# Row scatters of an expert-routing kernel issued in pairs and one by one, each behind a semaphore

## The chip, the cores and the metric

The kernel runs on one core of one Trainium2 chip. The metric is the device time of one execution in microseconds (us). A core has five engines with an instruction queue each: TensorE (PE: matmuls and transposes, with the weight loads shown as PEld), VectorE (DVE), ScalarE (ACT), GpSimd (POOL) and SyncE (SP, which here only issues plain DMAs). Engines wait for each other through semaphores.

## The reference, cut to what matters

```python
h = tok(x)                                      # patches of x times W, plus b: 128 x 92 tokens of 128
h = h + attention(layernorm(h), Wq, Wk, Wv, Wlt)
t = layernorm(h)
gates = softmax(t @ Wr + br)                    # 8 experts
top_vals, top_idx = top_k(gates, 2)             # two experts for each token, weights made to sum to 1
out = zeros_like(t)
for e in range(8):
    y = relu(t @ W1[e] + b1[e]) @ W2[e] + b2[e] # 128 -> 512 -> 128
    out = out + combine[:, e:e + 1] * y         # combine is zero but for a token's two experts
h = h + out
```

There are T = 11,776 tokens of D = 128 floats.

## The kernel before

It has four stages, one behind the other.

**Stage one** embeds and makes the attention, group by group.

**Stage two** walks over 23 chunks of 512 tokens (`NCH`). A chunk's eight blocks of attention output are turned by TensorE into four PSUM banks (`turn_a`, L1743), copied by ScalarE (`keep_aTh`, L980, semaphore `aTh_kept`), of six of them VectorE makes the rounding rest (`keep_aTl`, L1248), and TensorE projects them (L401 to L403, L1752). VectorE adds the residual (`keep_h1`, L1258; the trace calls its result `h`), TensorE turns the result to token rows with the router's columns beside it (`turn_h`, L1764), ScalarE keeps logits, residual and squares, GpSimd takes the power -1/2 of the variance (`root2`, L828, semaphore `rstd2_kept`), and VectorE does some 25 small routing steps that end in `posi`, the row of each token's two copies in an array sorted by expert. GpSimd then scatters the normalised rows `trow` to that array in DRAM (`scatter`, L835): eight indirect DMAs for a chunk (two choices times four row blocks), each of 128 rows. While chunk c is routed, TensorE already projects chunk c+1, and the scatters under way are those of chunk c-1.

**Stage three** walks over 53 tiles (`TILES`) of 512 sorted rows, seven of them of 256 rows (`HALF_TILES`). For each, `turn_tile` (L1780) and `keep_x`, `low_x` bring the rows in, `first_layer` makes four pieces of the hidden layer, ScalarE keeps each piece's high half (`keep_hid`, L1028) and VectorE its low half (`low_hid`, L1391, semaphore `hidl_kept`, four for a tile), `second_layer` multiplies them, `turn_y` (L1845) turns the result, VectorE weighs it (`weigh_y`, L1540, the trace's `ytok`), and GpSimd scatters it by token (L862): four indirect DMAs for a tile, two for a half one. The second half of tile n's work on TensorE is interleaved with the first of tile n+1.

**Stage four** loads the two results of each token and adds them.

The order on every engine is the order of the code: nothing is scheduled. GpSimd's queue in a step of stage two is: scatters 0 and 1 of chunk c-1, `root2(c)`, scatters 2 to 7 of chunk c-1. `pool_waits` is a helper that makes GpSimd wait for the semaphores given and then counts up one of its own.

Of the kernel before, what the change touches and what calls it, by code (L numbers as in the profile page):

```python
# [19 lines left out]
FC = FF // P  # L20
# [19 lines left out]
NCH = T // CT  # L40
RT = CT // P
# [4 lines left out]
AC = H * D // P  # L46
# [34 lines left out]
READY = 9  # L81
BY_DVE = tuple(c for c in range(NCH) if c not in BY_TENSOR)
TABLE_SET = 9
assert 2 * T % TT == 0 and T % CT == 0 and GT <= 512 and HH * S == GT and H * S * D == S * H * D


def at_least(eng, sem, value):

    if isinstance(value, int) and value <= 0:
        return  # L90
    eng.wait_ge(sem, value)
# [10 lines left out]
def rows_of_tile(n):  # L102

    return HT // P if isinstance(n, int) and n in HALF_TILES else TR
# [21 lines left out]
def build(nc, x, tok_w, tok_b, wq, wk, wv, wlt, wr, br, w1, b1, w2, b2, out):  # L126
# [9 lines left out]
    with ExitStack() as ctx, nc.allow_non_contiguous_dma("biases once"):  # L136
# [3 lines left out]
        def sem(name):  # L140
            return ctx.enter_context(nc.semaphore(name))
# [31 lines left out]
        last = ExitStack()  # L173
# [25 lines left out]
        first = ExitStack()  # L199
# [163 lines left out]
        aT_done, aTh_kept, aTl_kept, proj_done, h1_kept = (sem(n) for n in (  # L363
            "aT_done", "aTh_kept", "aTl_kept", "proj_done", "h1_kept"))
        wrc_done, wrc_kept, lean_kept, square_kept, var2_kept, rstd2_kept, shift_kept = (sem(n) for n in (
            "wrc_done", "wrc_kept", "lean_kept", "square_kept", "var2_kept", "rstd2_kept", "shift_kept"))
        route, mask_kept, gap_kept, gapexp_kept, count_done, posi_kept = (sem(n) for n in (
            "route", "mask_kept", "gap_kept", "gapexp_kept", "count_done", "posi_kept"))
        trow_kept, res_done, res_kept, goal_kept = (sem(n) for n in (
            "trow_kept", "res_done", "res_kept", "goal_kept"))  # L370
# [9 lines left out]
        hid_done, hidh_kept, hidl_kept, part_done = (sem(n) for n in ("hid_done", "hidh_kept", "hidl_kept", "part_done"))  # L380
# [39 lines left out]
        def steps_second(eng, chunk):  # L420

            chunk(0, 0, 0, True)
            for n in range(NE // 2):
                chunk(2 * n + 1, n, 1, True)
                chunk(2 * n + 2, n + 1, 0, True)
            with eng.Fori(NE // 2, (NCH - 3) // 2) as i:
                chunk(2 * i + 1, i, 1, True)
                chunk(2 * i + 2, i + 1, 0, True)
            chunk(NCH - 2, (NCH - 3) // 2, 1, True)
            chunk(NCH - 1, (NCH - 1) // 2, 0, False)  # L430
# [14 lines left out]
        def is_tile(n):  # L445
            return not isinstance(n, int) or 0 <= n < TILES

        def pool_waits(*waits):


            for sm, v in waits:
                at_least(nc.gpsimd, sm, v)
            nc.gpsimd.sem_inc(passed, 1)
# [200 lines left out]
        def _(pool):  # L654
# [143 lines left out]
            def set_table():  # L798

                for ins in (pool.iota(thresholds[:], pattern=[[HT, UNITS]], base=0, channel_multiplier=0,  # L800
                                      allow_small_or_imprecise_dtypes=True),
                            pool.iota(full_no[:], pattern=[[1, FULLS]], base=0, channel_multiplier=0,
                                      allow_small_or_imprecise_dtypes=True),
                            pool.iota(half_no[:], pattern=[[1, HALVES]], base=0, channel_multiplier=0,
                                      allow_small_or_imprecise_dtypes=True),
                            pool.iota(to_split[:], pattern=[[-2, 3]], base=HALVES - 2, channel_multiplier=0,
                                      allow_small_or_imprecise_dtypes=True),
                            pool.iota(star_row[:], pattern=[[TT, STAR]], base=0, channel_multiplier=0,
                                      allow_small_or_imprecise_dtypes=True),
                            pool.memset(len_line[:, 0:SEGS], 0.0),  # L810
                            pool.memset(seg_start[:, SEGS:SEGS + 1], float(SPARE_ROW)),
                            pool.iota(seg_step[:].rearrange("o (a e) -> o a e", a=2), pattern=[[0, 2], [0, NE]], base=1,
                                      channel_multiplier=0, allow_small_or_imprecise_dtypes=True)):
                    ins.then_inc(table_set, 1)
                pool.wait_ge(table_set, TABLE_SET - 1)
                ins = pool.iota(seg_step[:, NE - 1:SEGS:NE], pattern=[[NE - 1, 2]], base=1 - NE, channel_multiplier=0,
                                allow_small_or_imprecise_dtypes=True)
                ins.then_inc(table_set, 1)

            def lay_spare(k):  # L820
                row = SPARE_ROW + k * TT
                pool.dma_start(sorted_dram[row:row + TT, :].rearrange("(p r) w -> p r w", p=P),
                               spare_rows[:, k]).then_inc(spares_in, 16)

            def root2(c, q):

                pool_waits((var2_kept, c + 1), (trow_kept, 2 * c - 2), (mask_kept, c - 1))
                nc.gpsimd.tensor_tensor(rstdB[:, q], varB[:], power[:], ALU.pow).then_inc(rstd2_kept, 1)  # L828

            def scatter(c, q, first, last):  # L830

                if first == 0:
                    pool_waits((trow_kept, 2 * c + 2), (posi_kept, c + 1))
                for choice, r in [(k // RT, k % RT) for k in range(first, last)]:
                    pool.indirect_dma_start(  # L835
                        out=sorted_dram, out_offset=bass.IndirectOffsetOnAxis(ap=posi[:, q, choice, r:r + 1], axis=0),
                        in_=trow[:, q, choice, r], in_offset=None).then_inc(scattered[q], 16)

            def chunk(c, i, q, more):

                after_first = not isinstance(c, int) or c > 0
                if after_first:
                    scatter(c - 1, 1 - q, 0, 2)
                root2(c, q)
                if after_first:
                    scatter(c - 1, 1 - q, 2, 2 * RT)
                if isinstance(c, int) and c < SPARE:
                    lay_spare(c)
                if isinstance(c, int) and c == NE:
                    set_table()  # L850

            steps_second(pool, chunk)
            scatter(NCH - 1, (NCH - 1) % 2, 0, 2 * RT)

            def tile(n, i, q):
                m = n - 1
                if is_tile(m):
                    b = (q - 1) % XRING
                    pool_waits((tile_in[b], 16 * ((m // XRING if isinstance(m, int) else i - int(q == 0)) + 1)),
                               (ytok_kept, m + 1))  # L860
                    for r in range(rows_of_tile(m)):
                        pool.indirect_dma_start(  # L862
                            out=y_dram, out_offset=bass.IndirectOffsetOnAxis(ap=tin[:, b, r, D:D + 1].bitcast(I32), axis=0),
                            in_=ytok[:, b % 2, r], in_offset=None).then_inc(y_out[b % 2], 16)

            tiles(pool, tile)

        @block.scalar
# [245 lines left out]
        def _(dve):  # L1114
# [246 lines left out]
            def nxt(ins):  # L1361
                lined[0] += 1
                ins.then_inc(ready_kept, 1)
                dve.wait_ge(ready_kept, lined[0])
# [4 lines left out]
            def choose_star():  # L1369

                dve.wait_ge(table_set, TABLE_SET)
                nxt(V.tensor_reduce(best[:, 0:1], held[:], AX_X, ALU.max))
# [551 lines left out]
```

## Time and profile before

| | |
|---|---|
| median of 3 runs | 1600.33 us (1600.16 to 1606.58) |
| span of the profiled execution, first to last instruction | 1622.7 us |
| TensorE busy | 1443.9 us (89%) |
| VectorE, ScalarE, GpSimd busy | 73%, 62%, 49% |

The profiled execution has no time of its own beside its span. The span is 22.4 us over the median of the unprofiled runs. Busy shares are means over four stages. A bracket at the end of a row of the timeline says how long the engine had been idle ahead of that instruction and what ended it.

### The profile page before, as it was taken

What the parts mean: (1) busy time and instruction counts of PE and PEld (TensorE: products, weight loads), DVE (VectorE), ACT (ScalarE), POOL (GpSimd) and SP (SyncE); (2) the same over time, 40 slices, a digit from 0 to 9 for tenths busy, and PEclk for the clock granted to TensorE, in tenths of its full rate; (3) what the DMA queues carried; (4) which work ended last, traced back from release to release, by engine and by line L of the source; (5) the groups of instructions that cost most, each with busy time, mean ns of one, the idle gap of its engine ahead of it and who ended that gap; (6) DMA issues with size and microseconds to landing.
All of it is one profiled execution on the core that took longest, in us unless ns stands there. A gap on an engine that the chain in (4) does not pass through costs nothing.

```text
span 1622.7 us, 31484 instructions
## 1 busy us (share of the span) xinstructions
PE 1443.9 (89%) x7812; PEld 1155.4 (71%) x7812; DVE 1184.5 (73%) x3231; ACT 1008.0 (62%) x2311; POOL 788.2 (49%) x888
## 2 busy tenths in 40 slices
PE   5999999999999999999988878787858899998894
PEld 4778888888888888888766656565646777777671
DVE  3988989989989988988957666556756455555455
ACT  2777878878878878878855655455534444444350
POOL 2674444444444444444416665555654445445451
PEclk8999999999999999999999998888979989999996
DMA  3422222222222222222366664546446666655579
GB/s 83 138 85 78 97 83 81 92 84 82 90 84 86 86 84 87 85 84 88 125 236 216 229 218 163 194 148 207 140 161 224 231 232 224 210 203 207 194 255 364
DMA packets 135458, 245.74 MB, mean 151 GB/s; under 512 B 31536, under 2 KB 95552, under 8 KB 132448
## 3 DMA queue, kind: packets, MB, share of 16 engines
q1 hardware_dynamic: 114608, 206.57, 36.7%
q0 software_dynamic: 13920, 31.33, 5.8%
q10 hardware_dynamic: 6864, 7.09, 1.3%
q8 instruction: 27, 0.44, 0.1%
q14 instruction: 39, 0.32, 0.1%
HBM read 99.85 MB, written 89.51 MB: 117 GB/s over the span
## 4 chain that ended last, share of the span: by engine, by line
PE 73%; DVE 6%; issue 6%; another core or an unknown queue 5%; ACT 4%; DMA 2%; POOL 2%; SPq 1%; ACTq 0%; POOLq 0%; DVEq 0%
PE bank L401 15%; PE bank L403 14%; PE bank L402 13%; PE pair_ps L1678 9%; PE bank L1609 5%; PE bank L1703 4%; PE bank L1743 4%; PE pair_ps L1845 1%; PE pair_ps L1764 1%; PE bank L1599 1%; ACT trow L1003 1%; ACT aT_h L980 1%; PE bank L1752 1%; DMA yearly<-y_scratch 1%
## 5 line engine op out<-in xcount | busy, mean ns | idle before, releaser
L692 POOL TENSOR_TENSOR prob<-expo,inv 92x368 f32<-92x368 f32 x256 | 205.0, 801 | 394.4 <-DVE inv L1207 394.4
L862 POOL DMA_INDIRECT y_scratch<-ytok,tin x198 | 194.3, 981 | 189.5 <-issue 126.3
L835 POOL DMA_INDIRECT sorted_scratch<-trow,posi x184 | 180.2, 979 | 124.8 <-issue 87.2
L1678 PE MATMUL pair_ps<-z,xnT 128*92 128x368 f32 x512 | 201.4, 475 | 0.0
L1391 DVE SCALAR_TENSOR_TENSOR hid_l<-bank,hid_h 128x512 fp32r<-128x512 f32 (+1 forms) x159 | 103.7, 655 | 118.7 <-ACT hid_h L1028 69.3
L1200 DVE TENSOR_REDUCE peak<-pair_ps 92x4 f32<-92x368 f32 x256 | 136.1, 532 | 73.1 <-PE pair_ps L1678 72.9
L1248 DVE TENSOR_TENSOR aT_l<-bank,aT_h 128x512 fp32r<-128x512 f32 x138 | 94.9, 691 | 90.3 <-ACT aT_h L980 67.4
L902 ACT ACTIVATE z<-bank 128x368 f32<-128x368 f32 x254 | 121.2, 477 | 63.3 <-PE bank L403 56.0
L1028 ACT ACTIVATE hid_h<-bank 128x512 fp32r<-128x512 f32 (+1 forms) x159 | 90.6, 570 | 105.1 <-PE bank L403 73.9
L941 ACT ACTIVATE w2s<-bank 128x368 fp32r<-128x368 f32 x256 | 122.5, 479 | 47.2 <-PE bank L403 42.4
L948 ACT ACTIVATE expo<-cent 92x368 f32<-92x368 f32 x256 | 130.4, 509 | 31.1 <-DVE cent L1212 28.2
L1227 DVE TENSOR_TENSOR w2s<-bank,w2s 128x368 fp32r<-128x368 f32 x256 | 136.2, 532 | 5.9 <-ACT w2s L941 3.0
L1212 DVE TENSOR_TENSOR cent<-pair_ps,peak 92x368 f32<-92x368 f32 x256 | 136.4, 533 | 1.0
L1220 DVE TENSOR_TENSOR probT_l<-bank,probT_h 92x368 fp32r<-92x368 f32 x256 | 134.9, 527 | 1.8 <-ACT probT_h L929 1.8
L980 ACT ACTIVATE aT_h<-bank 128x512 fp32r<-128x512 f32 x138 | 83.7, 609 | 81.2 <-PE bank L1743 46.6
L1193 DVE TENSOR_REDUCE total<-expo 92x4 f32<-92x368 f32 x256 | 133.4, 521 | 0.4 <-ACT expo L948 0.3
L957 ACT ACTIVATE val<-bank 128x368 f32<-128x368 f32 x256 | 120.6, 471 | 17.0 <-PE bank L403 12.8
L1743 PEld LDWEIGHTS bank<-ident,arow 128*128 128x128 f32 x736 | 98.4, 151 | 42.1 <-issue 27.0
L401 PE MATMUL bank<-probT_h,xtok_h 92*128 92x368 f32 x256 | 114.1, 446 | 10.4 <-DVE w2s L1227 7.3
L1703 PE MATMUL bank<-ident,prob 92*92 92x92 f32 x1024 | 123.0, 242 | 0.3 <-POOL prob L692 0.3
L929 ACT ACTIVATE probT_h<-bank 92x368 fp32r<-92x368 f32 x256 | 119.7, 468 | 0.3
L1743 PE MATMUL bank<-ident,arow 128*128 128x128 f32 x736 | 119.4, 290 | 0.0
(274 smaller groups left out, 3972.7 us busy)
## 6 DMA issues: line engine op xcount, KB each, us to landing
ax_scratch<-val SPq DMA_DIRECT2D x64, 736.0 KB, 3.5
arow<-ax_scratch SPq DMA_DIRECT2D x23, 2048.0 KB
w1t<-w1s SPq DMA_DIRECT2D x53, 512.0 KB
w2t<-w2s SPq DMA_DIRECT2D x53, 512.0 KB
tin<-sorted_scratch SPq DMA_DIRECT2D x46, 260.0 KB
xin<-in_x_dram SPq DMA_DIRECT2D x32, 372.0 KB
ywide<-y_scratch SPq DMA_DIRECT2D x32, 256.0 KB, 6.7
h_scratch<-hP SPq DMA_DIRECT2D x32, 184.0 KB, 5.1
```

Of the source, the lines that this page charges most:

```text
L401: mm(dst, wh, vh, start=start, stop=False)
L402: mm(dst, wh, vl, start=False, stop=False)
L403: return mm(dst, wl, vh, start=False, stop=stop)
L692: nc.gpsimd.tensor_tensor(prob[:, k % 2], expo[:, k % 2], inv[:, k % 2].unsqueeze(2).to_broadcast([S, HH, S]), ALU.mult).then_inc(prob_kep ...
L835: pool.indirect_dma_start(out=sorted_dram, out_offset=bass.IndirectOffsetOnAxis(ap=posi[:, q, choice, r:r + 1], axis=0), in_=trow[:, q, ch ...
L862: pool.indirect_dma_start(out=y_dram, out_offset=bass.IndirectOffsetOnAxis(ap=tin[:, b, r, D:D + 1].bitcast(I32), axis=0), in_=ytok[:, b % ...
L1200: V.tensor_reduce(peak[:, k % 2], sc, AX_X, ALU.max).then_inc(peak_kept, 1)
L1212: V.tensor_tensor(cent[:, k % 2], sc, peak[:, k % 2].unsqueeze(2).to_broadcast([S, HH, S]), ALU.subtract).then_inc(cent_kept, 1)
L1227: V.tensor_tensor(mix_l[:, half * HH:(half + 1) * HH, b, :], mix_ps[:, 0:GT].rearrange("d (h i) -> d h i", h=HH), mix_h[:, half * HH:(half ...
L1678: mm(score_ps[k % 2][0:S, 0:GT], xnT[:, q, b * S:(b + 1) * S], z[:, b, half * HH:(half + 1) * HH, :], start=True, stop=True).then_inc(scor ...
L1703: ins = nc.tensor.transpose(probT_ps[kt % 2][0:S, m * S:(m + 1) * S], prob[:, kt % 2, m], ident[0:S, 0:S])
L1743: ins = nc.tensor.transpose(turn_ps[j % TURNS][:, r * P:(r + 1) * P], arow[q][:, r, j * P:(j + 1) * P], ident[:])
```

## The change

Every `scatter` after the first of a chunk now waits for something, and a chunk's last six are cut in three pairs:

```diff
@@ -81,6 +81,7 @@
+NEXT_LOW = {1: 0, 2: 1, 3: 2}
@@ -827,30 +828,36 @@
-            def scatter(c, q, first, last):
-
-                if first == 0:
-                    pool_waits((trow_kept, 2 * c + 2), (posi_kept, c + 1))
+            def scatter(c, q, first, last, *after):
+
+                pool_waits(*(after if first else ((trow_kept, 2 * c + 2), (posi_kept, c + 1))))
                 for choice, r in [(k // RT, k % RT) for k in range(first, last)]:
                     pool.indirect_dma_start(
                         out=sorted_dram, out_offset=bass.IndirectOffsetOnAxis(ap=posi[:, q, choice, r:r + 1], axis=0),
                         in_=trow[:, q, choice, r], in_offset=None).then_inc(scattered[q], 16)
 
             def chunk(c, i, q, more):
+
+                def turned(blocks):
+                    blocks += AC * (c + 1)
+                    return aTh_kept, min(blocks, AC * NCH) if isinstance(c, int) else blocks
 
                 after_first = not isinstance(c, int) or c > 0
                 if after_first:
                     scatter(c - 1, 1 - q, 0, 2)
                 root2(c, q)
                 if after_first:
-                    scatter(c - 1, 1 - q, 2, 2 * RT)
+                    scatter(c - 1, 1 - q, 2, 4, (rstd2_kept, c + 1))
+                    scatter(c - 1, 1 - q, 4, 6, turned(AC))
+                    scatter(c - 1, 1 - q, 6, 8, turned(AC + 1))
...
             steps_second(pool, chunk)
-            scatter(NCH - 1, (NCH - 1) % 2, 0, 2 * RT)
+            for k in range(0, 2 * RT, 2):
+                scatter(NCH - 1, (NCH - 1) % 2, k, k + 2, (hidl_kept, FC + k // 2))
@@ -859,6 +866,8 @@
                     for r in range(rows_of_tile(m)):
+                        if r in NEXT_LOW and is_tile(n + 1):
+                            pool_waits((hidl_kept, FC * (n + 1) + NEXT_LOW[r]))
                         pool.indirect_dma_start(
                             out=y_dram, out_offset=bass.IndirectOffsetOnAxis(ap=tin[:, b, r, D:D + 1].bitcast(I32), axis=0),
                             in_=ytok[:, b % 2, r], in_offset=None).then_inc(y_out[b % 2], 16)
```

`AC` is 8, the blocks of a chunk: `turned(AC)` is the moment when ScalarE has kept all eight blocks of chunk c+1, `turned(AC + 1)` that when it has kept the first of chunk c+2. `FC` is 4: `FC * (n + 1)` low halves are all of tile n, so a tile m = n - 1 has its second scatter behind the last low half of tile n, its third and fourth behind the first and second of tile n+1. No instruction of any other engine changes.

GpSimd's queue in the last two steps of stage two, of before (`trow` are the rows, `sorted_scratch` the sorted array, `rstdB` the result of `root2`):

```order
L835 DMA sorted_scratch<-trow,posi 101888x130 [waits trow_kept,posi_kept]
L835 DMA sorted_scratch<-trow,posi 101888x130
L828 TENSOR_TENSOR rstdB<-varB,power 128x4 [waits mask_kept,var2_kept,trow_kept]
L835 DMA sorted_scratch<-trow,posi 101888x130 x6
L835 DMA sorted_scratch<-trow,posi 101888x130 [waits trow_kept,posi_kept]
```

and of the same step in the changed kernel:

```order
L835 DMA sorted_scratch<-trow,posi 101888x130 [waits trow_kept,posi_kept]
L835 DMA sorted_scratch<-trow,posi 101888x130
L829 TENSOR_TENSOR rstdB<-varB,power 128x4 [waits mask_kept,var2_kept,trow_kept]
L835 DMA sorted_scratch<-trow,posi 101888x130 [waits rstd2_kept]
L835 DMA sorted_scratch<-trow,posi 101888x130
L835 DMA sorted_scratch<-trow,posi 101888x130 [waits aTh_kept]
L835 DMA sorted_scratch<-trow,posi 101888x130
L835 DMA sorted_scratch<-trow,posi 101888x130 [waits aTh_kept]
L835 DMA sorted_scratch<-trow,posi 101888x130
L835 DMA sorted_scratch<-trow,posi 101888x130 [waits trow_kept,posi_kept]
```

The instructions stand in the same order; the run of six without a wait has become three pairs with a wait each.

GpSimd's queue where stage two ends and the tiles begin, of before (`ytok` are a tile's weighed rows, `y_scratch` the array of results by token):

```order
L835 DMA sorted_scratch<-trow,posi 101888x130 [waits trow_kept,posi_kept]
L835 DMA sorted_scratch<-trow,posi 101888x130 x7
L862 DMA y_scratch<-ytok,tin 31232x128 [waits tile_in0,ytok_kept]
L862 DMA y_scratch<-ytok,tin 31232x128 x3
L862 DMA y_scratch<-ytok,tin 31232x128 [waits tile_in1,ytok_kept]
```

and of the changed kernel:

```order
L835 DMA sorted_scratch<-trow,posi 101888x130 [waits trow_kept,posi_kept]
L835 DMA sorted_scratch<-trow,posi 101888x130
L835 DMA sorted_scratch<-trow,posi 101888x130 [waits hidl_kept]
L835 DMA sorted_scratch<-trow,posi 101888x130
L835 DMA sorted_scratch<-trow,posi 101888x130 [waits hidl_kept]
L835 DMA sorted_scratch<-trow,posi 101888x130
L835 DMA sorted_scratch<-trow,posi 101888x130 [waits hidl_kept]
L835 DMA sorted_scratch<-trow,posi 101888x130
L871 DMA y_scratch<-ytok,tin 31232x128 [waits tile_in0,ytok_kept]
L871 DMA y_scratch<-ytok,tin 31232x128 [waits hidl_kept] x3
L871 DMA y_scratch<-ytok,tin 31232x128 [waits tile_in1,ytok_kept]
```

The last chunk's eight scatters, one run of before, now stand in pairs behind low halves of tile 1, and each of a tile's later scatters has a wait of its own.

## Rows read from the trace of the kernel before

**Rows 1.** Single lines: count, shortest, median and longest ns, first and last start.

```profile
L835 POOL DMA_INDIRECT sorted_scratch<-trow,posi x184: 965/972/1070, 851.6 to 1205.9; - x184
L1258 DVE TENSOR_TENSOR h<-bank,hch x23: 680/682/692, 836.9 to 1175.1; 128x512 f32<-128x512 f32 x23
L1540 DVE TENSOR_TENSOR ytok<-pair_ps,tin x53: 415/681/693, 1202.2 to 1582.6; 128x512 f32<-128x512 f32 x46, 128x256 f32<-128x256 f32 x7
```

**Rows 2.** Timeline, first chunks: start, us, engine, line, operation.

```profile
846.49 1.02 PE L1752 MATMUL bank<-aT_f,wlt_f 128*128 128x512 f32 x2
848.24 0.68 DVE L1258 TENSOR_TENSOR h<-bank,hch 128x512 f32<-128x512 f32 x1
```

**Rows 3.** Timeline of a later chunk, its scatters and what waits.

```profile
984.42 0.68 DVE L1258 TENSOR_TENSOR h<-bank,hch 128x512 f32<-128x512 f32 x1
...
988.96 0.97 POOL L835 DMA_INDIRECT sorted_scratch<-trow,posi  x1 [0.30 <-issue]
...
990.75 1.00 PE L1743 MATMUL bank<-ident,arow 128*128 128x128 f32 x4
...
991.79 0.60 ACT L980 ACTIVATE aT_h<-bank 128x512 fp32r<-128x512 f32 x1 [0.78 <-PE bank L1743]
...
992.75 1.02 POOL L835 DMA_INDIRECT sorted_scratch<-trow,posi  x1 [0.20 <-issue]
...
995.20 0.60 ACT L980 ACTIVATE aT_f<-bank 128x512 f32<-128x512 f32 x1 [0.53 <-issue]
...
996.55 0.60 PE L1743 MATMUL bank<-ident,arow 128*128 128x128 f32 x4
...
996.99 1.02 PE L1752 MATMUL bank<-aT_f,wlt_f 128*128 128x512 f32 x2
...
999.18 0.97 POOL L835 DMA_INDIRECT sorted_scratch<-trow,posi  x1 [0.30 <-issue]
1000.04 0.60 ACT L980 ACTIVATE aT_h<-bank 128x512 fp32r<-128x512 f32 x1 [2.43 <-PE bank L1743]
...
1001.41 0.69 DVE L1258 TENSOR_TENSOR h<-bank,hch 128x512 f32<-128x512 f32 x1
...
1002.34 2.17 PE L1764 MATMUL pair_ps<-turnw,h 128*128 128x137 f32 x8 [3.26 <-DVE h L1258]
```

**Rows 4.** Timeline where stage two ends: the last scatter of a row of twelve, and ScalarE.

```profile
1211.02 0.97 POOL L862 DMA_INDIRECT y_scratch<-ytok,tin  x1 [0.30 <-issue]
1211.96 0.60 ACT L1028 ACTIVATE hid_h<-bank 128x512 fp32r<-128x512 f32 x1 [7.19 <-remote]
```

**Rows 5.** Timeline of an undisturbed tile: weighed rows, a low half, the last scatter.

```profile
1345.32 0.68 DVE L1540 TENSOR_TENSOR ytok<-pair_ps,tin 128x512 f32<-128x512 f32 x1
...
1349.13 0.69 DVE L1391 SCALAR_TENSOR_TENSOR hid_l<-bank,hid_h 128x512 fp32r<-128x512 f32 x1 [0.68 <-ACT hid_h L1028]
...
1350.61 0.97 POOL L862 DMA_INDIRECT y_scratch<-ytok,tin  x1 [0.30 <-issue]
...
1351.72 0.68 DVE L1540 TENSOR_TENSOR ytok<-pair_ps,tin 128x512 f32<-128x512 f32 x1
```

**Rows 6.** Timeline of a disturbed tile.

```profile
1409.18 0.40 PE L403 MATMUL pair_ps<-x_both,w1t 128*128 128x512 f32 x1
...
1409.43 0.69 DVE L1540 TENSOR_TENSOR ytok<-pair_ps,tin 128x512 f32<-128x512 f32 x1
...
1410.92 0.96 POOL L862 DMA_INDIRECT y_scratch<-ytok,tin  x1 [1.12 <-issue]
...
1411.62 0.60 ACT L1028 ACTIVATE hid_h<-pair_ps 128x512 fp32r<-128x512 f32 x1 [3.12 <-PE bank L403]
...
1414.74 0.97 POOL L862 DMA_INDIRECT y_scratch<-ytok,tin  x1 [0.30 <-issue]
...
1416.04 0.69 DVE L1391 SCALAR_TENSOR_TENSOR hid_l<-bank,hid_h 128x512 fp32r<-128x512 f32 x1 [1.51 <-issue]
...
1419.36 0.68 DVE L1540 TENSOR_TENSOR ytok<-pair_ps,tin 128x512 f32<-128x512 f32 x1
```

## The prediction, made before the changed kernel ran

> **What bounds the kernel now.** I read the page, then single lines for the periods of the two loops, then the timeline around one chunk and two tiles. TensorE is busy for 89% of the span, so the question is what stops it in the rest. In stage two `keep_h1` ran 23 times from 836.9 to 1175.1 [rows 1], 338.2 / 22 = 15.4 us a chunk. Its first period, which held no scatter, took 848.24 - 836.9 = 11.3 us [rows 1, 2]. From there to the last are 326.9 us for 21 periods, 15.6 us each, 4.2 us over the first. In stage three `ytok` ran 53 times from 1202.2 to 1582.6 [rows 1], while an undisturbed tile takes 1351.72 - 1345.32 = 6.40 us [rows 5]. With 45 full periods at 6.4 and 7 half ones at 3.2, halved as the width is, the floor is 310 us for 380.4: 70 us over.
>
> The timeline shows where a chunk loses it. At 984.42 to 1001.41 (17.0 us) TensorE's last projection ends by its record at 996.99 + 1.02 = 998.01, and the `h` that waits for it starts at 1001.41, 3.4 us late; TensorE then had been idle 3.26 us when `turn_h` began. The turned block that ends at 996.55 + 0.60 = 997.15 reaches ScalarE at 1000.04, with ScalarE idle for 2.43 us of that [rows 3]. Without scatters the same projection ends at 847.51 and `h` starts at 848.24, 0.7 us later [rows 2]. What is late is not the work but the word of it: two engines that wait for TensorE are released together long after its record ends. GpSimd was in a run of six scatters, first at 992.75, last at 999.18 [rows 3], one each 1.28 us (0.97 and a gap of 0.30); `h` starts 2.2 us after the last one's start. Behind a pair nothing is late: the second scatter of a pair starts at 988.96, the block turned until 991.75 is taken up at 991.79 [rows 3]. Stage three has the same picture: a row of twelve scatters ends with that of 1211.02, and ScalarE stands 7.19 us until 1211.96 [rows 4]; `L403` ends by its record at 1409.58, ScalarE takes it up at 1411.62 [rows 6], 2.0 us late, behind a run of four. So I read: **after several scatters in close order TensorE's signals come late, until about 2.2 us after the last scatter starts; after two they don't.** The profile shows it as coincidence in time, not as a cause.
>
> **The change part by part.** The same 382 scatters are issued, of 0.972 us each [rows 1]. No data moves differently. What is added are waits and a count on GpSimd, three a chunk and up to three a tile. Its queue has room: it is busy for 49% of the span. Where a wait is already met it costs a queue instruction that hides behind the running scatter. Where it binds, the restart costs more: `ytok` ends at 1410.12 and its scatter starts at 1410.92 [rows 6], 0.8 us, against 0.30 between two in a run, so 0.5 us a binding wait, on an engine with slack. Behind a waiting scatter on GpSimd stand the chunk's other scatters and the next `root2`, for which ScalarE and VectorE wait a third of a period later.
>
> Chunk, pair two (behind `root2`): its wait is for the instruction just ahead, so I cost it at nothing, 0.5 us at most. Pair three, behind the last block kept: `aT_f` of 995.20 ends at 995.80 [rows 3], so it starts at 996.6 where its first scatter stands at about 995.35 by that spacing: 1.2 us later, and a gap of 2.5 instead of 1.3 in the run. Pair four waits for the block that ScalarE took at 1000.04; if the signal isn't late, that block is kept by about 998.3 (ScalarE is free at 1000.04 - 2.43 = 997.61, plus 0.60), and the pair starts at 999.1 instead of 997.90; if it is late, the run has stopped after four and the release comes 2.2 us after the fourth's start of 997.9, so at 1000.1 instead of 1001.4. Either way `h` can start earlier: by 1.3 us at least by that rule, and by 1001.41 - 998.8 = 2.6 us when nothing is late (0.7 us behind 998.01, as in [rows 2]). Above lies the whole excess of 4.2 us a chunk, below nothing, if the last pair, now next to the following chunk's first pair, makes a run of four with it and gives the gain back there. I take 1.5 us, near the lower of the two: the last pair still falls near `turn_h`. For 21 chunks **31 us** (0 to 88).
>
> The last chunk's scatters and tile 0's: the row of twelve goes. ScalarE's stop of 7.19 us becomes one of about 2: **5 us** (0 to 7).
>
> Tiles: in the undisturbed one the waits do nothing. The low half for which the fourth scatter would wait ends at 1349.13 + 0.69 = 1349.82; 0.8 us on is 1350.62, and the scatter starts at 1350.61 already [rows 5]. In the disturbed tile, 1409.43 to 1419.36 or 9.9 us, the fourth scatter started at 1414.74, while the low half it would wait for ended at 1416.73 [rows 6]: it would start at 1417.5, 2.8 us later, and the run of four, hard behind the one before, is broken up by waits that follow TensorE's own progress. I take it that a third to a quarter of the 70 us comes back: 3.5 us over the floor in such a tile, half of it regained, in some ten such tiles, 16 to 18: **16 us** (0 to 50, the rest belongs to the half tiles and to what starts a disturbance, which no wait touches).
>
> Sum 31 + 5 + 16 = 52 us off the profiled span of 1622.7, so 1571. The median stands 22.4 us under the span; I take the same 52 off it: **1548 us**. If late signals are shorter without the profiler, the gain is smaller; that stretches the range up.
>
> **The rivals.**
> *Smaller gain (1575 to 1592).* The signals stay late in most chunks: pairs two and three are still four scatters between 992.75 and 998.9, and pair four comes early in chunks at full clock. Then 0.5 to 1 us a chunk and little in the tiles: about 15 to 20 us, 1583.
> *No change (about 1600).* Late signals come from something else that happens to coincide, and the scatters merely stand nearby. For it speaks that no semaphore of GpSimd's is what TensorE waits for; against it, that chunks without scatters show none of it. Then only GpSimd waits longer: 1600. "Trainium Architecture — The Big Picture", section "What this means for kernel authors", in the Trainium skill says that the engines are independent and that one blocks another only through a semaphore, and that inside SBUF only VectorE and GpSimd share a port. By that rule a scatter can't delay TensorE's word to ScalarE, and the sum would be 0 and the time 1600. The trace speaks against it so far, with 3.4 us late behind six scatters and 0.7 us without.
> *Slower (about 1621).* The last pair of chunk c-1 now starts behind the first block of the next step, so around `h` of that step, and the first pair of chunk c follows `posi` some 2.5 us later: four in close order just where ScalarE waits for `turn_h` to make logits and squares. Those feed `root2`, and behind `root2` stand six scatters and all routing. If each chunk loses 1 us there beyond what it gains, that is 21 us: 1621. It decides from the point where the late word of `turn_h` costs more than the 3.4 us that `h` loses now. Against it: those two pairs are 2 us or more apart if the signal isn't late, and `turn_h` ends between them.
>
> **How the numbers follow.** Forecast, 1518 to 1575: 0.58. Smaller gain: 0.15. No change: 0.13. Slower: 0.14. A measurement of this kernel tells about 0.5% (8 us) from no change. The point is the forecast's, 1548. Its own range is 1518 to 1575, from 82 us off (two thirds of the 88 and a third of the 70) to 25. For 8 in 10 the range goes up to no change and leaves the slower case out: 1518 to 1602. Faster by over 0.5% takes the first two: 0.73; within 0.5% 0.13; slower 0.14.
>
> **What would show it.** In the changed kernel's profile: `keep_h1` less than 1.5 us behind TensorE's last projection in most chunks and a mean period of 14 us (23 starts in about 305 us); TensorE's granted clock less often halved in stage two, as its stops shrink; ScalarE's stop of 7 us at the stages' seam gone; tiles of over 9 us rare, and `ytok` from first to last in about 360 us; undisturbed tiles still 6.40. Wrong it would be if signals are as late with pairs as with six, if the lateness moves from `h` to the logits behind `turn_h`, or if unprofiled runs never had it.

## The result, and the profile after

The changed kernel took 1591.35 us (median of 20 runs, 1579.98 to 1598.63) where the kernel before took 1604.77 us in its 20 runs (1593.92 to 1614.0): a ratio of 0.992, 95% interval 0.990 to 0.994. So 13.4 us came back where 52 were forecast. It is faster, as forecast, but by a quarter of the amount, and outside the forecast's range of 1518 to 1575 us.

Two numbers of the forecast's ground look different now. The profiled execution of before that was read ahead of the prediction has a span of 1622.7 us, above every one of these 20 runs of before; a second profiled execution of the same kernel has 1597.6. And the profiled execution of after is the fastest of its 20. Comparing these two traces overstates the gain, so each kernel has a second trace below. The second traces come from two chips, on which the kernel before took 1601.29 (before_again's chip) and 1604.54 us (after_again's); on which chip the first trace of before was taken is not on record.

The page of the changed kernel, first lines (busy us, share of the span, instructions).

```profile
span 1578.2 us, 31768 instructions
PE 1421.0 (90%) x7812; PEld 1136.6 (72%) x7812; DVE 1181.5 (75%) x3231; ACT 1004.8 (64%) x2311; POOL 787.9 (50%) x888
```

Single lines of the changed kernel, beside [rows 1]. The diff moves the line numbers by 9 at `h` and `ytok`.

```profile
L835 POOL DMA_INDIRECT sorted_scratch<-trow,posi x184: 962/972/1068, 849.3 to 1196.1; - x184
L1267 DVE TENSOR_TENSOR h<-bank,hch x23: 678/680/681, 834.5 to 1168.2; 128x512 f32<-128x512 f32 x23
L1549 DVE TENSOR_TENSOR ytok<-pair_ps,tin x53: 411/681/693, 1190.6 to 1538.4; 128x512 f32<-128x512 f32 x46, 128x256 f32<-128x256 f32 x7
```

The scatters cost what they did. `h` runs over 333.7 us, 15.2 us a chunk, and `ytok` over 347.8. The same lines in the second traces, first of before, then of after:

```profile
L1258 DVE TENSOR_TENSOR h<-bank,hch x23: 680/681/692, 834.5 to 1158.3; 128x512 f32<-128x512 f32 x23
L1540 DVE TENSOR_TENSOR ytok<-pair_ps,tin x53: 415/681/692, 1184.9 to 1557.4; 128x512 f32<-128x512 f32 x46, 128x256 f32<-128x256 f32 x7
```

```profile
L1267 DVE TENSOR_TENSOR h<-bank,hch x23: 679/680/683, 839.2 to 1176.1; 128x512 f32<-128x512 f32 x23
L1549 DVE TENSOR_TENSOR ytok<-pair_ps,tin x53: 414/682/692, 1203.2 to 1552.6; 128x512 f32<-128x512 f32 x46, 128x256 f32<-128x256 f32 x7
```

In the second pair the chunks are slower with the change, 336.9 / 22 = 15.3 us against 323.8 / 22 = 14.7, and the tiles faster, 349.4 us against 372.5. In the first pair the chunks looked a little quicker (333.7 us against 338.2), because that trace of before is the longer of its two. Whether the two halves of the change pull against each other is tried below, one half at a time.

A chunk of the changed kernel (timeline, weight loads and small VectorE rows left out) shows where the chunk's loss stands.

```profile
995.71 0.97 POOL L835 DMA_INDIRECT sorted_scratch<-trow,posi  x1 [1.22 <-ACT aT_f L989]
996.98 0.97 POOL L835 DMA_INDIRECT sorted_scratch<-trow,posi  x1 [0.30 <-issue]
...
997.93 0.68 DVE L1267 TENSOR_TENSOR h<-bank,hch 128x512 f32<-128x512 f32 x1
998.26 0.96 POOL L835 DMA_INDIRECT sorted_scratch<-trow,posi  x1 [0.30 <-ACT aT_h L989]
...
998.85 1.17 PE L1773 MATMUL pair_ps<-turnw,h 128*128 128x137 f32 x8 [0.67 <-DVE h L1267]
...
999.53 0.97 POOL L835 DMA_INDIRECT sorted_scratch<-trow,posi  x1 [0.30 <-issue]
...
1001.28 0.96 POOL L835 DMA_INDIRECT sorted_scratch<-trow,posi  x1 [0.79 <-DVE posi L1355]
...
1002.55 0.97 POOL L835 DMA_INDIRECT sorted_scratch<-trow,posi  x1 [0.30 <-issue]
1003.01 0.20 ACT L995 ACTIVATE lgraw<-pair_ps 128x36 f32<-128x36 f32 x1 [4.75 <-remote]
...
1004.34 0.69 DVE L1257 TENSOR_TENSOR aT_l<-bank,aT_h 128x512 fp32r<-128x512 f32 x1 [3.21 <-remote]
...
1005.09 0.50 PE L402 MATMUL bank<-aT_h,wlt_h 128*128 128x512 f32 x1 [2.49 <-DVE aT_l L1257]
```

`h` no longer waits, and TensorE is idle for 0.67 us ahead of `turn_h`, where [rows 3] had 3.26. But `turn_h` ends by its record at 998.85 + 1.17 = 1000.02, and ScalarE takes it up (`lgraw`) at 1003.01, 3.0 us late, with ScalarE idle for 4.75 and VectorE for 3.21 us. The trace also holds the times at which semaphores are counted up: the count of `turn_h` comes at 1002.90. TensorE's next blocks start at 1000.56 and 1001.99, before that, so it is the word (the semaphore's count, which ScalarE waits for) that is late. The ends of matmuls in a profile are modelled, though; whether the last write of `turn_h` was late with its word no run here tells. Pairs three and four have run together to four scatters, 995.71 to 999.53, and the next chunk's first pair follows 0.79 us behind them. The late word has moved from `h` to the logits.

Where the tiles begin, ScalarE's longest stop is now 4.25 us where [rows 4] had 7.19 (timeline of the changed kernel, ScalarE alone):

```profile
1190.66 0.60 ACT L1037 ACTIVATE hid_h<-pair_ps 128x512 fp32r<-128x512 f32 x1 [3.44 <-PE pair_ps L404]
...
1199.65 0.60 ACT L1031 ACTIVATE x_both<-bank 128x512 fp32r<-128x512 f32 x1 [4.25 <-remote]
...
1203.99 0.60 ACT L1037 ACTIVATE hid_h<-pair_ps 128x512 fp32r<-128x512 f32 x1 [3.75 <-PE bank L404]
```

But only the first of the last chunk's pairs stands apart (same timeline, GpSimd alone):

```profile
1186.77 0.97 POOL L835 DMA_INDIRECT sorted_scratch<-trow,posi  x1 [0.30 <-issue]
1189.71 0.97 POOL L835 DMA_INDIRECT sorted_scratch<-trow,posi  x1 [1.98 <-DVE hid_l L1400]
1190.98 0.97 POOL L835 DMA_INDIRECT sorted_scratch<-trow,posi  x1 [0.30 <-issue]
1192.26 0.97 POOL L835 DMA_INDIRECT sorted_scratch<-trow,posi  x1 [0.30 <-issue]
...
1201.19 0.97 POOL L871 DMA_INDIRECT y_scratch<-ytok,tin  x1 [0.30 <-issue]
1205.36 1.09 POOL L871 DMA_INDIRECT y_scratch<-ytok,tin  x1 [3.20 <-DVE hid_l L1400]
```

The second pair waits for its low half, and by then the low halves of all that follow are there: from 1189.71 to 1201.19 ten scatters run 1.28 us apart, the other six of the chunk and tile 0's four. The row of twelve has become two and ten. The first four periods of `ytok`, which hold this place, take 38.8 and 38.0 us in the two traces of before and 35.7 in both of the changed kernel.

An undisturbed tile still takes 1488.96 - 1482.56 = 6.40 us, with its scatters now 1.60, 1.27 and 1.27 us apart (timeline, `ytok` and scatters of one tile):

```profile
1482.56 0.68 DVE L1549 TENSOR_TENSOR ytok<-pair_ps,tin 128x512 f32<-128x512 f32 x1
...
1484.02 0.97 POOL L871 DMA_INDIRECT y_scratch<-ytok,tin  x1 [1.25 <-issue]
...
1485.62 0.97 POOL L871 DMA_INDIRECT y_scratch<-ytok,tin  x1 [0.64 <-issue]
...
1486.89 0.97 POOL L871 DMA_INDIRECT y_scratch<-ytok,tin  x1 [0.30 <-issue]
...
1488.16 0.97 POOL L871 DMA_INDIRECT y_scratch<-ytok,tin  x1 [0.31 <-issue]
...
1488.96 0.68 DVE L1549 TENSOR_TENSOR ytok<-pair_ps,tin 128x512 f32<-128x512 f32 x1
```

Of the 52 periods from `ytok` to `ytok` 3 are over 8.5 us, where the two traces of before have 13 and 17.

### The profile page after: what moved, and what is told of

Its sections match the earlier page's. It is cut to its first block, busy times and chain, and to the rows that moved or that the text cites. A ratio compares the mean times of both kernels' runs of the same rounds, so it can differ in the third digit from the quotient of the medians.

```text
span 1578.2 us, 31768 instructions
## 1 busy us (share of the span) xinstructions
PE 1421.0 (90%) x7812; PEld 1136.6 (72%) x7812; DVE 1181.5 (75%) x3231; ACT 1004.8 (64%) x2311; POOL 787.9 (50%) x888
## 4 chain that ended last, share of the span: by engine, by line
PE 73%; DVE 8%; issue 7%; ACT 4%; another core or an unknown queue 4%; DMA 2%; POOL 1%; SPq 1%; ACTq 0%; DVEq 0%; POOLq 0%
PE bank L402 16%; PE bank L404 14%; PE bank L403 14%; PE pair_ps L1687 9%; PE bank L1618 5%; PE bank L1712 5%; PE bank L1752 3%; PE pair_ps L1854 1%; PE bank L1608 1%; ACT trow L1012 1%; PE bank L1789 1%; ACT aT_h L989 1%; DMA yearly<-y_scratch 1%; DVE aT_l L1257 1%
## 5 line engine op out<-in xcount | busy, mean ns | idle before, releaser
L402 PE MATMUL bank<-aT_h,wlt_h 128*128 128x512 f32 x138 | 73.1, 530 | 54.2 <-DVE aT_l L1257 41.8
```

What stands on the lines that cost most here:

```text
L402: mm(dst, wh, vh, start=start, stop=False)
```

## The experiments

Two kernels are no experiments but second looks at before and after, for the reading above. Each ratio is to runs of the kernel before that were taken with it.

**before_again.** 

> The kernel before, unchanged, for a second trace. If the first trace (span 1622.7 us) is a typical execution, chunks again take 15.4 us and ytok again runs over about 380 us. If it is an unusually slow one, which its distance to the median says, the span is about 1603 us and the difference lies in the tiles or the chunks: ytok from first to last in 360 to 370 us.

It took 1599.37 us, with a span of 1597.6, 25 us under the first trace. The chunks make up 14 of these; `ytok` from first to last, 372.5 us, lies a little above what was expected.

**after_again.** 

> The changed kernel again, for a second trace: h about 0.8 us behind the last projection, logits over 4 us behind h, chunks 15.2 us or more, ytok from first to last 345 to 360 us; span 1585 to 1595 us.

It took 1594.63 us (span 1592.8), and all else came as expected: `h` 0.8 us behind the last projection, the logits 4.6 us behind `h`, chunks of 15.3 us, tiles in 349.4.

**One half of the change at a time.** In chunks_only, tiles and last chunk scatter as before; in tiles_only, the chunks do:

```diff
 # chunks_only keeps these two places as before
-            for k in range(0, 2 * RT, 2):
-                scatter(NCH - 1, (NCH - 1) % 2, k, k + 2, (hidl_kept, FC + k // 2))
+            scatter(NCH - 1, (NCH - 1) % 2, 0, 2 * RT)
...
-                        if r in NEXT_LOW and is_tile(n + 1):
-                            pool_waits((hidl_kept, FC * (n + 1) + NEXT_LOW[r]))
 # tiles_only keeps this one as before
-                    scatter(c - 1, 1 - q, 2, 4, (rstd2_kept, c + 1))
-                    scatter(c - 1, 1 - q, 4, 6, turned(AC))
-                    scatter(c - 1, 1 - q, 6, 8, turned(AC + 1))
+                    scatter(c - 1, 1 - q, 2, 2 * RT)
```

**chunks_only.** 

> Only the waits of stage two's chunks; last chunk and tiles as before. Theory A: GpSimd's scatters are worked off slower (about 1.5 us each) than a run issues them (1.28 us), TensorE's signals wait behind a run of three and more, and the pairs of the change close up to such runs again at another place, so the lateness moved from h to the logits. Then the chunks take 15.0 to 15.3 us and the time is 0 to 5 us under the kernel before (ratio 0.997 to 1.000). Theory B: the pairs gain in the chunks as forecast and the tiles are what gave it back: ratio 0.98.

**tiles_only.** 

> Only the waits of the last chunk and of the tiles; the chunks as before. Theory A: nearly all of the measured 13 us is here: ratio 0.991 to 0.995, ytok from first to last about 350 us in the profile. Theory B: no gain here: ratio 1.000 or above.

Measured: chunks_only 1616.86 us against 1601.29, ratio 1.008 (1.005 to 1.011). tiles_only 1574.42, ratio 0.983 (0.979 to 0.988). Single lines of `h` and `ytok`, first chunks_only, then tiles_only:

```profile
L1264 DVE TENSOR_TENSOR h<-bank,hch x23: 680/681/682, 838.5 to 1178.6; 128x512 f32<-128x512 f32 x23
L1546 DVE TENSOR_TENSOR ytok<-pair_ps,tin x53: 415/681/693, 1205.5 to 1579.4; 128x512 f32<-128x512 f32 x46, 128x256 f32<-128x256 f32 x7
```

```profile
L1266 DVE TENSOR_TENSOR h<-bank,hch x23: 680/681/692, 836.4 to 1163.6; 128x512 f32<-128x512 f32 x23
L1548 DVE TENSOR_TENSOR ytok<-pair_ps,tin x53: 415/681/692, 1186.4 to 1531.9; 128x512 f32<-128x512 f32 x46, 128x256 f32<-128x256 f32 x7
```

By these ratios the chunks' part costs 0.8%, 12.5 us (the interval says 8 to 18), and the tiles' part with the last chunk's gives 1.7%, 27 us (20 to 34). Together 14.5, which fits the 13.4 measured: the two halves do pull against each other. Neither expectation had chunks_only slower than before, and tiles_only was expected to gain half as much. tiles_only alone beats both kernels.

**Spacing alone, in the order of before.** Behind every scatter, in chunks and tiles, GpSimd clears a small tile of its own, which nobody reads; order and waits stay those of before. The whole output is computed.

```diff
+            def space(done):
+                pool_waits((idled, done))
+                pool.memset(idle[:], 0.0).then_inc(idled, 1)
...
                         in_=trow[:, q, choice, r], in_offset=None).then_inc(scattered[q], 16)
+                    space(2 * RT * c + RT * choice + r)
```

The tile has 160 floats in spaced, 280 in spaced_mid, 400 in spaced_wide and 640 in spaced_more.

**spaced.** 

> The kernel before with no wait of the change; instead GpSimd clears 160 floats of one partition (about 0.25 us) behind every scatter, so that scatters start 1.5 to 1.6 us apart instead of 1.28 and their order and place stay. Theory A (they are worked off in about 1.5 us each, and the signals are late only when they pile up): no late signals, undisturbed tiles of 6.4 us throughout, chunks of about 14 us bounded by GpSimd, 1540 to 1570 us. Theory C (each scatter delays signals whatever its distance, or their number counts): the same lateness over a longer run of scatters, chunks of 17 us, 1610 to 1640 us.

**spaced_mid.** 

> The scatters' order of before, with a memset of 280 floats behind each scatter, for starts about 1.46 us apart, between the 1.37 us of the kernel spaced (ratio 0.990) and the 1.56 us of spaced_wide (0.968). Theory (each scatter is worked off in about 1.47 us, and a run issued faster than that builds a backlog behind which TensorE's signals wait): the backlog all but vanishes at 1.46, so most of the gain is there, 0.970 to 0.978, 1556 to 1569 us. Rival (the gain only follows the spacing evenly, with no point at which it turns): halfway between the two, 0.979, 1571 us. Rival (a run of six is late because it is one run, unless it is slower by more than the DMA's own time): as spaced, 0.988 to 0.992.

**spaced_wide.** 

> As spaced, but GpSimd clears 400 floats, 0.42 us by the 0.22 us that 160 took. In spaced the starts came 1.37 us apart, closer than 1.47 us, in which the trace shows a scatter of a run worked off (runs of six released 8.75 us after their start at spacings of 1.28 and of 1.37 alike). Now they come about 1.56 us apart. Theory A: nothing piles up, TensorE's signals are late by under 0.5 us, chunks take about 13.5 us, undisturbed tiles 6.40 us, no tile over 8.5 us; 1535 to 1560 us. Theory C (the number of scatters in a row counts, whatever their spacing): the lateness stays and lasts 9.4 us a run; chunks 15 us, 1590 to 1610 us.

**spaced_more.** 

> The same with a memset of 640 floats, starts about 1.75 us apart. Theory: there is no backlog to take away beyond 1.56 us, so the ratio stays at 0.965 to 0.972, unless GpSimd itself becomes late: eight scatters then take 14.0 us, which is the whole period of a chunk (13.8 us), so routing and root2 are late and a chunk takes 14.5 to 15 us: 1565 to 1580 us, ratio 0.975 to 0.985. I take the latter. Rival (gain grows evenly with spacing): 0.95, 1524 us.

Measured, with the start to start of two scatters of a run:

| | spacing | us | ratio (95%) | a chunk | `ytok`, first to last |
|---|---|---|---|---|---|
| before_again | 1.28 | 1599.37 | | 14.7 | 372.5 |
| spaced | 1.37 | 1586.88 | 0.990 (0.986 to 0.993) | 14.0 | 378.7 |
| spaced_mid | 1.47 | 1577.96 | 0.985 (0.981 to 0.990) | 14.2 | 360.7 |
| spaced_wide | 1.56 | 1551.97 | 0.968 (0.964 to 0.972) | 13.8 | 342.2 |
| spaced_more | 1.77 | 1590.02 | 0.994 (0.991 to 0.997) | 15.3 | 349.9 |

spaced was expected at 1540 to 1570 us, and missed it: its clears set the scatters only 1.37 us apart, not 1.5 to 1.6. With 1.56 us, in spaced_wide, GpSimd was given more to do and the kernel got 3.2% faster. Timeline of spaced_wide, around one `h`:

```profile
1007.22 0.98 POOL L841 DMA_INDIRECT sorted_scratch<-trow,posi  x1 [0.17 <-POOL idle L834]
...
1008.20 0.42 POOL L834 MEMSET idle<- 1x400 f32 x1
...
1008.45 0.68 DVE L1267 TENSOR_TENSOR h<-bank,hch 128x512 f32<-128x512 f32 x1
1008.79 0.97 POOL L841 DMA_INDIRECT sorted_scratch<-trow,posi  x1 [0.17 <-POOL idle L834]
...
1009.40 1.17 PE L1773 MATMUL pair_ps<-turnw,h 128*128 128x137 f32 x8 [0.51 <-DVE h L1267]
...
1010.35 1.01 POOL L841 DMA_INDIRECT sorted_scratch<-trow,posi  x1 [0.17 <-POOL idle L834]
1010.69 0.20 ACT L995 ACTIVATE lgraw<-pair_ps 128x36 f32<-128x36 f32 x1 [2.30 <-issue]
...
1021.62 0.29 PE L1779 MATMUL bank<-mask_line,before_r 128*128 128x40 f32 x1 [0.90 <-DVE upto L1327]
...
1022.41 0.68 DVE L1267 TENSOR_TENSOR h<-bank,hch 128x512 f32<-128x512 f32 x1
```

Scatters stand on both sides of `turn_h`, without any pause between them, and yet its end at 1010.57 reaches `lgraw` at 1010.69, 0.1 us later, where after had 3.0. So it is not how many scatters stand in a row, but how close. The upper end is another bound: spaced_more, expected at 0.975 to 0.985, came to 0.994. In it eight scatters of 1.77 and a `root2` of 1.0 make 15.2 us, which is its chunk (15.3; the expectation had the bound right and its size, 14.5 to 15, too small); and its `ytok` waits for the scatters themselves to land, 36 times, where before_again's did once (a line of spaced_more, and what its engine waited for, us and times):

```profile
L1549 DVE TENSOR_TENSOR ytok<-pair_ps,tin x53: 415/692/694, 1197.6 to 1547.5; 128x512 f32<-128x512 f32 x46, 128x256 f32<-128x256 f32 x7
...
  DMA y_scratch<-ytok,tin: 76.9, 36
```

In spaced_wide the same sum is 8 x 1.56 + 1.0 = 13.5 of 13.8 us: its chunks too stand near GpSimd's own bound. spaced_mid's expectation of 0.970 to 0.978 was missed: at 1.47 its third to eighth periods take 13.5 to 13.7 us, later ones 12.9 to 19.6. At that spacing the late words come and go. Nor does the gain follow the spacing evenly: from 1.28 to 1.47 it is 1.5%, from there to 1.56 another 1.7%.

**How often the word is late.** Each recorded count of a semaphore of TensorE's can be set against the end of the last matmul before it that counts that semaphore up. Before the first scatter there are 1474 such counts in each trace, and none comes over 0.02 us behind the matmul's end. In the chunks (first scatter to last `h`) and the tiles (first to last scatter of `ytok`):

| | chunks: counts | over 1 us late | tiles: counts | over 1 us late |
|---|---|---|---|---|
| before_again | 309 | 89 | 398 | 77 |
| after_again | 328 | 89 | 387 | 53 |
| late_pair | 296 | 11 | 411 | 76 |
| spaced_mid | 293 | 52 | 413 | 71 |
| spaced_wide | 304 | 1 | 380 | 51 |
| spaced_more | 344 | 0 | 414 | 0 |

Of the counts by ScalarE, VectorE and GpSimd none is over 0.1 us late in these two stretches of any of the six traces. So only TensorE's words are held up. The changed kernel has as many late ones in its chunks as the kernel before, and fewer in its tiles; and at 1.56 us the chunks are clear of them, the tiles not yet.

**The last pair moved away.** late_pair is chunks_only with the last pair of chunk c-1 behind the logits of chunk c+1 instead of the first turned block of chunk c+2. It has no clear in it: where it has fewer late words, order alone takes them away.

```diff
-                    scatter(c - 1, 1 - q, 6, 8, turned(AC + 1))
+                    scatter(c - 1, 1 - q, 6, 8, (lean_kept, min(c + 2, NCH) if isinstance(c, int) else c + 2))
```

**late_pair.** 

> chunks_only with the last pair moved on: it waits for the next chunk's logits (lean_kept) instead of its first turned block, so it no longer lies between h and the logits. If what chunks_only gave back was the late word of turn_h, then h stays about 0.8 us behind the last projection, the logits come 2 to 3 us behind h instead of 4.5, and the time falls from 1617 to 1590 to 1600 us. Rival: wherever the pair stands it makes a run of four with the first pair and another word is late; then h and logits are prompt and the chunks still take over 15 us, 1605 to 1625 us.

Measured 1590.08 us, ratio 0.990 (0.987 to 0.993), where chunks_only had 1.008. One wait moved, same scatters, 1.8% of the time. `h` in late_pair:

```profile
L1264 DVE TENSOR_TENSOR h<-bank,hch x23: 678/680/686, 839.3 to 1149.0; 128x512 f32<-128x512 f32 x23
```

That is 14.1 us a chunk against 15.5, with the tiles as slow as before (375.8 us). The time and the logits, 2.4 us behind `h`, came as expected; `h` did not stay 0.8 us behind the last projection, it stands 2.5 behind it, for the reason given under the next table.

**Waits and spacing together.** both is tiles_only with the 400 floats behind the chunks' scatters alone; wide_tiles has them behind the tiles' too; after_wide is the changed kernel with them behind all.

**both.** 

> The change's waits for the last chunk and the tiles (tiles_only), and in the chunks no wait but 400 floats cleared behind each scatter. Theory A: chunks of 13.5 us instead of 14.9 in tiles_only, so some 30 us under tiles_only: 1540 to 1550 us. Theory C: 1575 us or more.

**after_wide.** 

> The changed kernel, all its waits kept, with the memset of 400 floats behind each scatter (starts 1.56 us apart in a run). Theory (the changed order loses in the chunks only through the backlog of the four scatters that come together around turn_h): with the backlog gone the order hardly matters, so the chunks fall to about 13.8 to 14.0 us and the time is that of spaced_wide or both, 1550 to 1565 us, ratio 0.967 to 0.975. Rival (the changed order is bad by itself, because its waits keep root2 and routing behind them): chunks stay near 15 us, 1575 to 1585 us, ratio 0.983 to 0.988.

**wide_tiles.** 

> The chunks' order of before with the memset of 400 floats behind every scatter (chunks and tiles), and the changed kernel's waits in the tiles and for the last chunk. Theory (order in the chunks costs, waits in the tiles gain, spacing takes away most of the rest): the chunks of spaced_wide (13.8 us each) with the tiles of after_wide (335 us from the first to the last ytok), so 342.2 - 335.4 = 7 us under spaced_wide, about 1545 us, ratio 0.963 to 0.967, the fastest of all. Rival (with the spacing the waits in the tiles have nothing left to do): as spaced_wide, 0.968 to 0.972.

Measured: both 1558.48 us, ratio 0.973 (0.969 to 0.977), expected at 1540 to 1550, its chunks at 13.8 us and no quicker than spaced_wide as a whole; after_wide 1560.69, 0.975 (0.970 to 0.980); wide_tiles 1558.28 on a chip where before took 1615.07, ratio 0.963 (0.959 to 0.967), the lowest of all, though its interval overlaps that of spaced_wide. Its ratio is the expected one, but the time is not the expected 1545 us, since that chip is a slower one, and the parts are not either: in its trace the chunks take 14.0 us and the tiles 350.1 us, not 335. That the waits add something to the spacing is therefore likely and not shown. after_wide's time is in its expected range, but its chunks take 14.5 us, not 13.8 to 14.0: the changed order keeps a cost of 0.7 us a chunk even without late words, probably since its waits lengthen a GpSimd queue that is nearly full; no run separates this. Its tiles are the shortest, 335.4 us.

**Where a chunk's time goes.** From the starts and ends in each trace, means over 21 chunks, in us: from `h` to `lgraw`; from there to the end of TensorE's last projection; from there to the next `h`.

| | `h` to `lgraw` | to last projection | to next `h` | sum |
|---|---|---|---|---|
| before_again | 3.8 | 9.3 | 1.8 | 14.9 |
| chunks_only | 4.5 | 10.3 | 0.8 | 15.7 |
| after_again | 4.6 | 10.1 | 0.8 | 15.5 |
| late_pair | 2.4 | 9.4 | 2.5 | 14.2 |
| spaced_wide | 2.4 | 9.1 | 2.5 | 14.0 |

With nothing late `h` to `lgraw` is 1.97, as in the first chunk. chunks_only wins 1.0 us over before in the third column and loses 0.7 and 1.0 in the others: the lateness that the waits take from `h` stands at the blocks and logits around it. The 2.5 us of the last two kernels are no late word: VectorE has `h` behind the routing, and the routing waits for `root2`, which GpSimd starts 2.5 us (late_pair, median) and 2.0 us (spaced_wide) behind its input, where it was 0.3 before. TensorE's wait for `upto`, a step of the routing, at 1021.62 above is the sign of it.

## Why the prediction was half right

- **"After several scatters in close order TensorE's signals come late"**: right, and now shown by spacing alone, against the rival of no change: GpSimd's scatters do delay TensorE's word here, by 3.0 us in the row of `lgraw` above, and 3.2% hang on their spacing. The Trainium skill, "Trainium Architecture — The Big Picture", section "What this means for kernel authors", says that the engines are independent and that one blocks another only where a semaphore stands between them. These runs don't agree: GpSimd's scatters hold up TensorE's word with no semaphore of theirs in between, and in before_again's chunks 89 of 309 counts come over 1 us late.
- **"Until about 2.2 us after the last scatter starts; after two they don't"**: this rule was the weak one. The two engines of [rows 3] are not released together either, but at 1000.04 and 1001.41. Counted from the start of a run, the words of [rows 3] come at 1000.04 - 992.75 = 7.29 and at 1001.41 - 992.75 = 8.66 us; in the changed kernel at 1003.01 - 995.71 = 7.30. That is about five and six times 1.46. Runs of six at 1.28, 1.37 and 1.47 us mostly release their last late word 8.6 to 9.2 us from the start, so 2.2 us behind the last start is only what 1.28 leaves. What fits is a backlog: each scatter is worked off in some 1.46 us and issued every 1.28, and a late word comes when one of them is done. An idle of 0.79 us between two pairs does not clear it. How much backlog holds a word up is not shown, and that late words still come at 1.47 us does not follow from it.
- **Chunks, "I take 1.5 us": the step that failed.** The gain at `h` was there, 0.8 us behind the last projection, within the "less than 1.5" asked for, in 20 of 21 chunks. What I set aside as a rival ("four in close order just where ScalarE waits for `turn_h`") happened: the logits start over 1 us behind the end of `turn_h` in 16 of 23 chunks of the changed kernel. The reading of one late chunk hid that they were late in 10 of 23 of the kernel before, in the same trace, by up to 5.0 us, mostly in chunks where `h` is prompt. Against it I had written that "those two pairs are 2 us or more apart", and their starts are 1.75 apart (999.53 and 1001.28), with no gap that counts. Forecast 31 us of gain, measured 12.5 of loss (chunks_only); late_pair, which takes the last pair out of there, turns it into a gain of 1.0%.
- **Last chunk and tiles, 5 + 16 us**: right in direction, too small. Measured 27 (tiles_only). `ytok` from first to last was forecast at about 360 and is 348 and 349. The seam was the smaller part: its row of twelve did not go but became ten, ScalarE's stop of 7 us became one of 4.25, not of 2, and the first four periods of `ytok` give 2 to 3 us. The rest came from the later tiles, a term that the sum had at 16, below its own "third to a quarter" of 70.
- **The baseline**: an excess of 88 and 70 us was read from an execution that is slower than any of the 20 timed ones. In before_again the chunks exceed 11.3 us by (14.9 - 11.3) x 21 = 76 and the tiles the floor of 310 by 62 us. The tiles' term and the upper bounds were scaled on ground that was some 20 us too high.
- **Mean chunk 14 us, clock less often halved**: neither came. The chunk is 15.2 and 15.3 us. Over all of stage two the granted clock is 0.90 and 0.94 of full speed in the two traces of before and 0.93 and 0.92 in those of the changed kernel (windows from the first to the last `h` of before, before_again, the changed kernel and after_again: us, then busy us of each engine, and PEclk, DMA share, GB/s):

```profile
836.90:1175.10 338.20, 269.57 (x1404) 209.96 (x1402) 220.88 (x864) 189.76 (x514) 190.56 (x204) 0.90 0.57 194
834.50:1158.30 323.80, 261.04 (x1404) 201.67 (x1402) 222.47 (x864) 188.93 (x514) 190.67 (x204) 0.94 0.59 203
834.50:1168.20 333.70, 266.24 (x1405) 202.22 (x1402) 219.17 (x864) 187.69 (x514) 190.55 (x205) 0.93 0.57 197
839.20:1176.10 336.90, 268.97 (x1405) 203.69 (x1402) 219.37 (x864) 187.44 (x514) 189.59 (x204) 0.92 0.56 194
```

Only the first pair of traces shows a rise. TensorE's stop ahead of `turn_h` has shrunk to 0.67 us and another has come in its place, that of 2.49 us behind the logits.

## What to carry to other kernels

When an engine takes up another's work long after its record ends, look for what a third engine issues in close order at that time, and test it by spacing those instructions, before any reordering. Count the late handovers of every kind over the whole loop, not in one chunk. A wait that moves work out of one critical place sets it down in another: write down which handover stands at the new place, here `turn_h` to `lgraw`. And before sizing a gain by the excess in one trace, see whether that execution stands within the timed runs.

## What the runs showed of the hardware

- Indirect scatters of 128 rows, issued 1.28 us apart by GpSimd, delay the words of TensorE to other engines, in before_again 89 of 309 in the chunks by over 1 us, and by up to 5.5 us in a chunk of the changed kernel (`turn_h` ends at 981.21, `lgraw` starts at 986.72). 1.56 us apart it is 1 of 304 in the chunks but 51 of 380 in the tiles, and 1.77 us apart none of 758. No count by another engine is over 0.1 us late in these stretches. A clear of 0.42 us behind each scatter (start to start 1.56) made the kernel 3.2% faster. What the words and the scatters share on the chip no run here tells: the backlog fits the release times, but it was inferred from them, and why at 1.47 us one chunk is free of it and the next not stays open.
- The same kernel's two profiled executions differ by 1622.7 - 1597.6 = 25 us, while the same kernel's 20 timed runs spread over 20. Chips differ too: on the three of the experiments the kernel before took 1601.03 and 1601.29 us (two sets of runs), 1604.54 us and 1615.07 us.
